# One layout for all edge rows, head rows freed by a copy, and a wider, earlier look-up in a two-hop graph attention kernel

## What is computed

```python
def _agg(ent, rel, head, tail, etype, fc_w, fc_b):
    a_input = concatenate([ent[head], ent[tail]], axis=-1)
    e = leaky_relu(sum((a_input @ fc_w.T + fc_b) * rel[etype], axis=-1), 0.2)
    m = segment_max(e, head); exp_e = exp(e - m[head])
    alpha = exp_e / segment_sum(exp_e, head)[head]
    return segment_sum(ent[tail] * alpha[:, None], head) + ent
for _ in range(2):
    ent = _agg(ent, ...); ent = ent / maximum(norm(ent), 1e-12)
out = layernorm(x + ent)
```

## Time and profile before

| | |
|---|---|
| median of 3 runs | 2926.75 us (2924.62 to 2942.11) |
| the profiled execution | 2912.71 us, its span 2910.3 us |
| POOL busy | 1780.5 us (61%) |
| DVE busy | 1850.1 us (64%) |
| PE / ACT busy | 1099.4 us (38%) / 860.1 us (30%) |
| mean granted TensorE clock | 0.58 of full speed |
| small DMA packets | 182810 of 235265 under 512 B |

### The profile page before, as it was taken

One profiled execution on the slowest core, in us unless ns is written; L12 is line 12 of the kernel. 1 busy time (PEld: TensorE's weight loads), 2 busy tenths in 40 slices (PEclk: granted clock), 3 DMA queues, 4 the chain that ended last, 5 costly groups with the idle time before them and its releaser, 6 DMA issues. The chain is left out here.

```text
span 2910.3 us, 22387 instructions
## 1 busy us (share of the span) xinstructions
PE 1099.4 (38%) x4597; PEld 839.1 (29%) x4597; DVE 1850.1 (64%) x3677; ACT 860.1 (30%) x1608; POOL 1780.5 (61%) x1607
## 2 busy tenths in 40 slices
PE   4688602233233233223322634343433434333310
PEld 4577601122132123222212423221222322222210
DVE  6967863366556556556636567775776668577684
ACT  2334312454455455445521211110111111011121
POOL 1000057277777777777764347777677767767776
PEclk9556555555555555555555556565665656556555
DMA  3455432366676676676664562222222222222110
GB/s 89 124 152 151 137 61 65 61 117 105 117 127 98 115 130 114 103 121 121 100 105 95 69 127 84 67 79 65 79 67 64 81 63 80 65 66 62 55 56 13
DMA packets 235265, 265.66 MB, mean 91 GB/s; under 512 B 182810, under 2 KB 190123, under 8 KB 231636
## 3 DMA queue, kind: packets, MB, share of 16 engines
q1 hardware_dynamic: 184804, 205.51, 32.4%
q0 software_dynamic: 50416, 59.64, 10.3%
HBM read 141.54 MB, written 128.15 MB: 93 GB/s over the span
## 5 line engine op out<-in xcount | busy, mean ns | idle before, releaser
L574 POOL DMA_INDIRECT area<-tail,gi x784 | 805.6, 1028 | 294.1 <-issue 241.3
L574 POOL DMA_INDIRECT area<-head,gi x392 | 465.6, 1188 | 277.2 <-DVE gi L1138 145.2
L623 POOL DMA_INDIRECT out<-area,place x392 | 493.6, 1259 | 119.4 <-issue 119.4
L764 PE MATMUL psR<-area,row_t 128*98 128x512 f16 (+1 forms) x896 | 301.2, 518 | 634.8 <-DVE area L1186 216.4
L672 PE MATMUL psP<-V,vT 65*125 65x40 f32 (+1 forms) x1586 | 317.3, 388 | 170.1 <-issue 65.3
L764 PEld LDWEIGHTS psR<-area,row_t 128*98 128x98 f16 x896 | 157.5, 184 | 772.0 <-issue 535.2
L672 PEld LDWEIGHTS psP<-V,vT 65*125 65x125 f32 (+1 forms) x1586 | 310.0, 304 | 188.2 <-issue 70.2
L664 PE MATMUL psT<-ident,area 128*65 128x128 f32 x393 | 90.1, 420 | 560.5 <-issue 495.4
L664 PEld LDWEIGHTS psT<-ident,area 128*65 128x65 f32 x393 | 80.2, 229 | 569.0 <-issue 569.0
L869 ACT ACTIVATE area<-iota_h,half_hi 128x392 f16<-128x392 f16 x392 | 237.8, 607 | 9.4 <-issue 9.4
L1137 DVE COPY gi<-head_i 128x14 int32 (+1 forms) x28 | 5.0, 180 | 347.1 <-DMA rows<-area 299.4
(11 more groups left out here) (267 smaller groups left out, 2460.0 us busy)
## 6 DMA issues: line engine op xcount, KB each, us to landing
area<-rows SPq DMA_DIRECT2D x28, 1183.0 KB
tail<-area SPq DMA_DIRECT2D x50, 637.5 KB
area<-tail_digits SPq DMA_DIRECT2D x28, 896.0 KB
rows<-area SPq DMA_DIRECT2D x28, 735.0 KB
tail<-area SPq DMA_DIRECT2D x28, 595.0 KB
area<-tail SPq DMA_DIRECT2D x25, 637.5 KB
head<-area SPq DMA_DIRECT2D x25, 630.0 KB
area<-tail,gi POOLq DMA_INDIRECT x784
```

The costliest lines, as they stand in the source:

```text
L574: pool.indirect_dma_start(out=to[:, b, k, 0:tab.shape[1]], out_offset=None, in_=tab, in_offset=bass.IndirectOffsetOnAxis(ap=gi[:, b, n, k: ...
L623: pool.indirect_dma_start(out=out, out_offset=bass.IndirectOffsetOnAxis(ap=place[:, b, k:k + 1].bitcast(U32), axis=0), in_=rowO[:, b, k, 0 ...
L764: last = te.matmul(psR[g % 2][0:HH, 0:w], row_t[:, n, c, :], hot_lo[:, c, 4 * g * P:4 * g * P + w], start=c == 0 and n == 0, stop=c == HB ...
```

## The change

- **Rows.** All rows have 105 words: channels, the one, both sets of 20 products. `rows0` takes the place of `tail0` and `head0`, `rows1` that of `tail1` and the old `rows1`. The heads' x lie in a table of their own, `head_xs` (64 words). A node chunk of the first stage takes 2 ACT copies and one store in place of 4 and two. The seam's two scatters become one, its three gathers four.
- **Head rows of hop 0.** ACT copies the heads' x into a new tile `rowX` (L926 of the changed kernel) right behind `decay`. DVE's `free()` waits for this copy; SP stores out of `rowX`, one contiguous piece for each partition; `dump` is one DMA of one contiguous piece.
- **Order in hop 0.** ACT copies the transposes of chunk j in chunk j+1, behind `decay` and the copy to `rowX`. PE counts ahead of `project`, no longer in halves. `row_table` stands ahead of chunk 25.
- **Look-up of hop 1.** `look_wide` puts the four groups in four PSUM banks, and the sums in a fifth; all four `choose` stand in the middle of DVE's chunk, the next one-hot tiles right behind them, and `take_rows` and the indices of chunk j+2 right behind the scan.
- **SP in hop 1.** It loads the head rows and `rowX` (two DMAs) when DVE counts `s_free`, behind the last use of the head rows.
- **PSUM operands in hop 1.** Intermediate values (`held*`) lie in PSUM, so that a two-input operation of DVE has a PSUM operand or result, but for the product (L1392) and the scan (L1394).

```diff
-    tail0 = dram("tail0", [N, WT])
-    head0 = dram("head0", [NPAD, WH])
-    tail1 = dram("tail1", [NPAD + N, WT])
-    rows1 = dram("rows1", [NPAD, W1])
+    rows0 = dram("rows0", [NPAD, WE])
+    rows1 = dram("rows1", [NPAD + N, WE])
+    head_xs = dram("head_xs", [NPAD, C])
...
+    wide_look = [psR[0], psR[1], psT[:, 0, :], psT[:, 1, :]]
+    held = flatP[:, 0:K * C].rearrange("p (k c) -> p k c", c=C)
...
-            def head_x(j, b, i):
-                sp.wait_ge(s_gat[b], 16 * 2 * K * (i + 1))
+            def head_x(j, b):
+                sp.wait_ge(s_xc, j + 1)
                 sp.sem_inc(s_turn_sp, 1)
-                sp.dma_start(re[:, cols(j), X0:W1], rowH[:, b, :, 0:C]).then_inc(s_xc[b], 16)
+                sp.dma_start(xe[:, cols(j), :], rowX[:, b, :, :]).then_inc(s_xst[b], 16)
...
-                sp.dma_start(re[:, cols(j), 0:X0], rowO[:, b, :, 0:X0]).then_inc(s_dump[b], 16)
-                sp.dma_start(te[:, cols(j), :], rowO[:, b, :, 0:WT]).then_inc(s_dump[b], 16)
+                sp.dma_start(re[:, cols(j), :], rowO[:, b, :, :]).then_inc(s_dump[b], 16)
...
-                    sp.wait_ge(s_idx, NCH + j + 1)
+                    if static:
+                        sp.wait_ge(s_idx, NCH + j + 1)
+                    else:
+                        sp.wait_ge(s_free, j - 1)
                     sp.dma_start(rowH[:, b, :, :], re[:, cols(j), :]).then_inc(s_hl[b], 16)
+                    sp.dma_start(rowX[:, b, :, :], xe[:, cols(j), :]).then_inc(s_hl[b], 16)
...
+            def look_wide(j):
+                pe.wait_ge(s_hot, j + 1)
+                pe.wait_ge(s_took, j * 4)
+                for g in range(4):
...
+                pe.wait_ge(s_took, j * 4 + 4)
+                pe.wait_ge(s_rank, j)
+                for k in range(K):
+                    last = te.matmul(psM[:, k:k + 1], chosen[0:HH, k * P:(k + 1) * P], ones[0:HH, 0:1], start=True, stop=True)
+                last.then_inc(s_sum, 1)
...
                     sc_.copy(decay[:, :, 1:K + 1], ex[:, 0:1, :].to_broadcast([P, CO, K])).then_inc(s_ex, 1)
+                    if h == 0:
+                        if not static:
+                            act.wait_ge(s_xst[b], 16 * i)
+                        sc_.copy(rowX[:, b, :, :], rowH[:, b, :, 0:C]).then_inc(s_xc, 1)
+                        if not (static and b == 0):
+                            copies(s_tr, (j - 1) * NB, s_trc, K, vT, P, s_act, CO)
...
                             projected(j - 1, 1 - b)
-                        copies(s_tr, j * NB, s_trc, K, vT, P, s_act, CO)
...
-                link(ve.tensor_tensor(vv, agg, wide(rd[:, 0:K0], K0), ALU.mult))
-                ve.tensor_tensor(vv, vv, rowsH[:, :, 0:C], ALU.add).then_inc(s_sq, 1)
+                via, rd_, rs_, mean_ = (vv, rd, rs, mean) if h == 0 else (held[:, 0:K0, :], held_rd, held_rs, held_mean)
+                link(ve.tensor_tensor(via, agg, wide(rd_[:, 0:K0], K0), ALU.mult))
+                ve.tensor_tensor(vv, via, rowsH[:, :, 0:C], ALU.add).then_inc(s_sq, 1)
...
+                    if taking and h == 1:
+                        take_rows(taking[0], psM[:, 0:K])
+                    if ahead and h == 1:
+                        dve.wait_ge(s_rank, j + 3)
+                        indices(j + 2, b, 1)
-                    link(ve.reciprocal(rd[:, :], S[:, C, 1:K + 1]))
+                    link(ve.reciprocal(rd_[:, :], S[:, C, 1:K + 1]))
...
                         if look:
-                            choose(look[0], range(2))
+                            choose(look[0], range(2 if h == 0 else 4))
+                        if after_look:
+                            hots(*after_look)
...
                     def free():
                         if ahead:
-                            if h == 0:
-                                dve.wait_ge(s_xc[b], 16 * (i + 1))
-                            indices(j + 2, b, h)
+                            dve.wait_ge(s_xc, j + 1)
+                            indices(j + 2, b, 0)
...
-                    if h == 0 and j == NCN - 1:
+                    if h == 0 and j == NCN:
                         row_table()
```

More of the change, by code:

```diff
@@ L313, in build_gnn @@
         s_pr = sem("rows_projected")
-        s_xc = [sem(f"head_x_stored{b}") for b in range(2)]
-        s_seam_x = sem("seam_x_copied")
+        s_xc = sem("head_x_copied")
+        s_xst = [sem(f"head_x_stored{b}") for b in range(2)]
         s_out = sem("projections_copied")
@@ L741, in project, with count @@
                 products(K, P, 2 * R, s_pr)
-            def count(j, static, half):
+            def count(j, static):
                 t0, n = counted(j, static)
                 s0 = t0 if static else 2 * MORE
-                for k in range(KS // 2) if half == 0 else range(KS // 2, n):
+                for k in range(n):
                     pe.wait_ge(s_sgn, t0 + k + 1)
@@ L755, in look @@
                 pe.sem_inc(s_turn_pe, 1)
-                if not (isinstance(j, int) and j == 0):
+                if j > 0:
                     pe.wait_ge(s_rank, j)
@@ L759, in look @@
                     w = min(4 * P, (K - 4 * g) * P)
-                    if not (isinstance(j, int) and j == 0 and g < 2):
+                    if j > 0 or g >= 2:
                         pe.wait_ge(s_took, j * 4 + g - 1)
@@ L770, in look @@
                 last.then_inc(s_sum, 1)
+            def look_wide(j):
+                pe.wait_ge(s_hot, j + 1)
+                pe.sem_inc(s_turn_pe, 1)
+                pe.wait_ge(s_took, j * 4)
+                for g in range(4):
+                    w = min(4 * P, (K - 4 * g) * P)
+                    for c in range(HB):
+                        for n in range(2):
+                            last = te.matmul(wide_look[g][0:HH, 0:w], row_t[:, n, c, :], hot_lo[:, c, 4 * g * P:4 * g * P + w],
+                                             start=c == 0 and n == 0, stop=c == HB - 1 and n == 1)
+                    last.then_inc(s_look, 1)
+                pe.wait_ge(s_took, j * 4 + 4)
+                pe.sem_inc(s_turn_pe, 1)
+                pe.wait_ge(s_rank, j)
+                for k in range(K):
+                    last = te.matmul(psM[:, k:k + 1], chosen[0:HH, k * P:(k + 1) * P], ones[0:HH, 0:1], start=True, stop=True)
+                last.then_inc(s_sum, 1)
             def first_hop(i, static):
                 for b in range(2):
-                    count(i * 2 + b, static, 0)
+                    count(i * 2 + b, static)
                     project(i * 2 + b, b)
-                    count(i * 2 + b, static, 1)
             pe.wait_ge(s_digc, 1)
@@ L1315, in _, with chunk @@
                 link(ve.memset(first[:, :], 0.0))
-                def chunk(j, b, static, ahead, i, nodes=h == 0, look=None, taking=None, h=h, nr=nr, r0=r0, e0=e0, x0=x0):
+                def chunk(j, b, static, ahead, i, nodes=h == 0, look=None, taking=None, after_look=None, h=h, nr=nr, r0=r0, e0=e0, x0=x0):
                     cc = cols(j)
                     H, Tl = rowH[:, b, :, :], rowT[:, b, :, :]
-                    if taking:
-                        take_rows(taking[0])
-                    if look:
+                    if taking and h == 0:
+                        take_rows(taking[0], psX)
+                    if look and h == 0:
                         hots(*look)
-                    link(ve.tensor_tensor(typ[:, :, :], iota_r[:, :].unsqueeze(1).to_broadcast([P, K, R]),
+                    if h == 1 and static and b == 0:
+                        hots(3, 1, 1)
+                    typ_, iota_ = (typ, iota_r) if h == 0 else (held_typ, held_iota)
+                    rd_, part_ = (rd, part) if h == 0 else (held_rd, held_part)
+                    link(ve.tensor_tensor(typ_[:, :, :], iota_[:, :].unsqueeze(1).to_broadcast([P, K, R]),
                                           wide(type_f[:, cc], K, R), ALU.is_equal))
@@ L1397, in pair @@
                         chunk(i * 2 + b, b, static, True, i, look=(q, 1 - b, i + 1 + b) if h == 1 else None,
-                              taking=(q - 1,) if h == 1 and not (static and b == 0) else None)
+                              taking=(q - 1,) if h == 1 and not (static and b == 0) else None,
+                              after_look=(q + 1, b, i + 2) if h == 1 else None)
                 link.base += link.n
```

225 lines of the change are left out of this document (116 added, 109 removed).

## The result

The changed kernel took 3009.09 us (median of 4 runs, 2981.79 to 3035.7) against 2925.68 us before: a ratio of 1.0202, interval 1.0109 to 1.0295. (The ratio compares fast executions alone, 2981.79 and 2988.95 us of the changed kernel, so it is smaller than that of the medians.) It was about 2% slower, where 2690 us was forecast, with a range of 2645 to 2800. The profiled execution took 2988.95 us, its span is 2986.9.

The account below looks back on a forecast made before the run. POOL was taken to bound both hops, pausing for DVE's indices. From 2912.7 us profiled, 110 (hop 0), 3 (rows) and 120 (hop 1) came off: 2680, plus 14 for the median, rounded to 2690 us; range 2645 to 2800.

Parts of the forecast that it names:

- POOL bounds both hops: Both hops: POOL's gathers, scatters and issue pauses fill periods of 42.6 and 42.7 us, with waits for DVE's indices.
- the last gather of hop 0: Sign to look for in the changed profile: hop 0's last gather near 1520.
- Head rows freed by a copy: Hop 0: DVE waits for an ACT copy, not a DMA landing, so POOL's index waits go; gain 110 us, bounds 58 to 133.
- The start-up stall: Hop 0's start: POOL's 50.5 us wait at 579, ACT standing for a semaphore; slack for ACT leaves 10 us of it.
- the stands around the row table: End of hop 0: POOL's waits of 28.6 and 13.2 us; with the table a chunk later, 8 of 41.8 us stay.
- The look-up behind the scan: Hop 1: sums taken behind the scan get some 15 us more, so POOL's 2.2 us of waits a chunk go.
- PSUM operands: Hop 1: PSUM operands relieve POOL of hold-ups by DVE's two-input operations; 2.5 of 4.9 us a chunk can go.
- the new period: Hop 1: POOL's gathers, scatters, issue pauses and 2.4 us of stalls make 37.8 us a chunk, against 42.7; gain about 120 us.
- rival 2: Hop 1: the look-up chain through PE, with late semaphores, becomes the bound; no gain there, 2810 us; chance 0.13.
- Rival 4: Hop 0: a POOL that never pauses blocks PE's signals and runs dry, 50 us seven times; 3030 us; chance 0.05.
- The Trainium skill's inference: Says two-SBUF-input DVE instructions don't stall descriptor generation, so PSUM operands would free nothing; the prediction went against it.

Follow-up runs that it names:

- a_copy: Changed kernel, unaltered, as a control beside the kernel before; PE's signals on time: 0.934 of before, 2657.8 us.
- b_few: Kernel before with fewer PE semaphore increments in hop 0 (one for four counts, one for a chunk's transposes); signals on time: 1.000 of before, 2846.8 us.
- b_more: Kernel before with 8 further PE semaphore increments, awaited by nobody, in each look-up of hop 1; signals on time: 1.000 of before, 2880.1 us.
- a_land: Changed kernel, but in hop 0 DVE waits for the landing of SP's rowX store, not ACT's copy; signals on time: 0.921 of before, 2656.2 us.
- b_psum: Kernel before with the PSUM operands of hop 1 alone; signals on time: 0.964 of before, 2773.7 us.
- b_psum2: Kernel before with the PSUM operands of hop 1 alone, measured once more; signals late: 1.038 of before, 3106.0 us.
- a_sbuf2: Changed kernel with all operands of hop 1 back in SBUF, measured a second time; signals late: 0.956 of before, 2861.3 us.
- a_small: Changed kernel with the small operands of hop 0 in a free PSUM bank in chunks 0 to 24; signals on time: 0.907 of before, 2615.8 us.
- a_copy2: Changed kernel, unaltered, a second control beside the kernel before; signals on time: 0.920 of before, 2653.6 us.
- a_best: Changed kernel with small operands of hop 0 in PSUM and a third of PE's semaphore increments; signals late: 1.021 of before, 2977.9 us.
- a_pause: Changed kernel, but POOL waits ahead of each chunk's scatters in hop 1 until PE has signalled the next look-up; signals late: 0.953 of before, 2854.1 us.

## Why the prediction was wrong, by its own steps

*POOL bounds both hops.* Right on time: POOL never waits there, the seam's scatter to the last one took 1064 us in a_copy (1058 + 6 forecast), at 37.9 us a chunk against 37.8, and the last gather of hop 0 came at 1520, as forecast.

*Head rows freed by a copy, 110 us.* On time the first gather to the seam's scatter fell from 1285 (b_few) and 1321 (b_more) to 1193 (a_copy), 92 to 128 us. The size was right, the reason in part: DVE's wait for the landing was there (280.4 us in 17 times in b_few, 600 to 1400) and is gone, but a_land shows that with the dense store the place of the wait is worth nothing. The prediction listed the dense store and gave it no price.

*The start-up stall, 10 us left of 50.* It is no trait of the program: in b_psum, b_more and b_few, whose hop 0 is that of before, POOL stands 11 us there on time, and 54 in b_psum2 when late. What I priced as ACT's slack was late signals. Likewise the stands around the row table, 28.6 and 13.2 us, are 10.5 and 14.4 in b_more on time, and none in a_copy.

*The look-up behind the scan, 2.2 us a chunk.* On time it is worth nothing (b_psum and a_copy both 1064 to 1065 us), since the kernel before doesn't wait there either (b_few and b_more: POOL never waits for indices in 1800 to 2500). When late it may be worth something: 1194 us before, 1163 in a_sbuf2, but these are of different groups.

*PSUM operands, 2.5 us a chunk.* Right and larger on time: 98 to 104 us in place of 70. That they cost DVE nothing shows too: the product for `cap` takes 1.12 us with a PSUM operand (L1410) and 1.11 with both in SBUF (L1367 before).

*The total on time.* 2654 to 2658 us lie inside the range, near 2690, and that is in part luck: 2690 counts the late kernel's stands as gains, which on time were mostly not there to be gained, while the start is lower there (2846 to 2884 us before) and the relief of POOL was larger than forecast.

*The step that failed* is the new period, "14 × 0.944 + 14 × 0.984 + 28 × 0.30 + 2.4 = 37.8 us": it has no term for a wait for PE's signals at L1219, and takes POOL's hold-ups as pure loss. The runs showed 47.7 us in its place, with DVE waiting at L1219 for look-ups made up to 45 us before. The sums did come in time (L1225 has no wait from "remote" between 1900 and 2800). I had rows of signals that came late while POOL issued, and priced them as a delay of up to 14.8 us, which the new order could bear (rival 2: 31 us against 37.8). It is no fixed delay. It grew to 45 us in a schedule where DVE hardly holds POOL up, and b_psum2 shows that the PSUM operands turn from a gain into a loss when signals are late. Rival 4 came nearest to the mechanism ("if signals from PE don't get through while POOL issues without pause") but put it in hop 0, and had 0.05; rival 2 had the place, L1219, and 0.13. Together they are near to what happened. Hop 1 took 1295 us in place of 1064, which is 231 of the 309 us by which the profiled execution (2989) missed 2680; most of the rest is hop 0, whose last gather came at 1593.5 in place of 1520.

*The Trainium skill's inference* (SBUF — State Buffer, § Who interferes with whom) that a two-input DVE operation does not stall descriptor generation is contradicted here: b_psum's and a_small's gains are such hold-ups removed (scatters of hop 1 from 1196 to 1087 ns, gathers of hop 0 from 1140 to 1069).

## What stays open

Why the signals are late in some measurements and not in others is not known: whole groups of runs were of one kind. It is no fixed trait of a chip, by the chip numbers on record: these put the on-time group of a_copy2 and the late group of a_best on the chip of the same number, some ten minutes apart. What in POOL's issuing stands in the way isn't shown either.

That a stand of POOL lets signals through was tried (a_pause). The traces agree: of the 59 late semaphore events of hop 1 of the changed kernel (those with no end of a PE instruction within 0.06 us), 28 came while POOL stood, which is 19% of the time. But 23 came while it issued undisturbed, so a stand isn't needed. That DVE's hold-ups let signals through is inferred from a_sbuf2 and b_psum2, and the traces support it only in part: 25 of 59 late events of hop 1 before came during instructions of POOL that DVE held up (over 1.1 us; 27% of the time), 86 of 141 in hop 0 before (25%), but 44 of 113 in a_sbuf2 (31%) and 60 of 240 in hop 0 of the changed kernel (23%), not far from what chance would give. A rival that no run excludes is that DVE's accesses to PSUM make PE's signals later in a way of their own, without POOL. A kernel of PSUM operands in both hops with such stands in hop 0 was not tried, nor was the changed kernel unaltered ever measured in the late groups of the experiments: its only late measurement is the result.

## What to carry to other kernels

Stalls of one engine may be what another's signals live on: before removing them, look who waits by "remote" while that engine runs, and ask when the wait ended, not only how long it was. A delay read in one schedule is no constant: up to 14.8 us of waiting before became 45 us from signal to arrival where POOL paused less. Measure a change on more than one occasion, with an unaltered control in each, before naming its cause: here one edit looked like a 12% cure only because the control was missing.

## What the runs showed of the hardware

- Where late, a count raised by PE reached DVE up to 45 us after it was made while POOL issued indirect DMAs, at times between POOL's undisturbed gathers (2334.01 in the timeline of the result), and some 3 to 5 us after POOL's last one where it fell idle (a_pause, result). Where on time, the gap was some 0.01 us under the same issuing.
- A DVE operation with both inputs in SBUF holds POOL's issue up (2.46 us in place of 0.98); with one of them in PSUM the hold-up is gone, as b_psum shows over 700 us of hop 1 (means of 1087 and 1005 ns in place of 1196 and 1183).
- A store of 448 KB lands in 2.5 us out of a dense tile into a dense table (a_land), in 9.2 us in pieces of 256 bytes out of and into wider rows (b_few).
- An indirect gather costs POOL 0.944 us in the median with 85 words and with 105 (all gathers of the kernel after: least/median/most ns):

```profile
L588 POOL DMA_INDIRECT area<-rows,gi x1176: 940/944/2307, 380.4 to 2916.0; - x196
```
